# Dense gate weights and a ones row by transfer, and attention values projected per head ahead of the tail

## What is computed

```python
for l in range(4):                       # sLSTM: a recurrence over 256 time steps, 4 layers x 4 heads of 32
    x = x + slstm_layer(ln(x, ln1_w[l]), conv_w[l], conv_b[l], wi[l], wf[l], wz[l], wo[l], rker[l], ...)
    x = x + gelu_ffn(ln(x, ln2_w[l]), ff_up[l], ff_down[l])

q = (x @ Wq).reshape(B, Nq, 16, 64)      # cross attention: 16 heads of 64, 6404 keys of 96 channels
k = (context @ Wk).reshape(B, Nk, 16, 64)
v = (context @ Wv).reshape(B, Nk, 16, 64)
attn = softmax(einsum('bqhd,bkhd->bhqk', q, k) * scale)
out = einsum('bhqk,bkhd->bqhd', attn, v).reshape(B, Nq, 1024) @ Wo + bo

for e in range(8):                       # top-1 routed experts with a capacity
    h = relu(tokens @ W1[e] + b1[e]); y = h @ W2[e] + b2[e]
```

## Time and profile before

| | |
|---|---|
| three runs, median | 4427.65 us |
| profiled execution | 4419.72 us (span 4418.0 us) |
| TensorE busy | 3766.4 us, 85% |
| VectorE busy | 3524.0 us, 80% |
| ScalarE busy | 2774.5 us, 63% |
| GpSimd busy | 1048.1 us, 24% |
| preamble, until the last of its instructions | 52.5 us |
| 10 plain chunks | 67.6 to 832.4 us |
| 28 chunks with attention | 836.2 to 3190.4 us |
| tail, 16 heads | 3289.0 to 4332.8 us |

### The profile page before, as it was taken

How to read it: one execution, slowest core, us unless ns; L and a number is a source line. 1 busy time by engine, 2 the same in 40 slices (tenths; PEclk the granted TensorE clock), 3 DMA queues, 4 the chain that set the end, 5 groups by cost and what they waited for, 6 DMA issues and landing times. The chain is left out here.

```text
span 4418.0 us, 103873 instructions
## 1 busy us (share of the span) xinstructions
PE 3766.4 (85%) x37640; PEld 2179.4 (49%) x37640; DVE 3524.0 (80%) x15928; ACT 2774.5 (63%) x8980; POOL 1048.1 (24%) x1219
## 2 busy tenths in 40 slices
PE   4666666459999999999999999999869999999997
PEld 2433334335445444444544544544426666666666
DVE  6777777688888888888888888888667877877865
ACT  3555555435666666666666666666617777777774
POOL 1000000000000000000000000000038788888883
PEclk7555555558999999999999999999969999999998
DMA  3111111000000000000000000000031121122100
GB/s 85 36 42 40 38 43 35 8 4 2 2 5 2 2 3 3 3 4 3 2 2 4 2 2 3 2 2 3 2 89 32 39 47 36 35 47 44 27 9 25
DMA packets 63160, 90.32 MB, mean 20 GB/s; under 512 B 11284, under 2 KB 58196, under 8 KB 59540
## 3 DMA queue, kind: packets, MB, share of 16 engines
q1 hardware_dynamic: 59468, 79.31, 7.2%
q10 hardware_dynamic: 3176, 4.36, 0.4%
HBM read 53.61 MB, written 28.82 MB: 19 GB/s over the span
## 5 line engine op out<-in xcount | busy, mean ns | idle before, releaser
L1201 PEld LDWEIGHTS G<-st,rec_w 128*128 128x128 f16 x19456 | 606.2, 99 | 960.3 <-DVE st L1372 925.0
L1201 PE MATMUL G<-st,rec_w 128*128 128x1 f16 x19456 | 683.4, 165 | 406.9 <-DVE st L1372 390.2
L1629 POOL TENSOR_TENSOR plt<-pft,pht 128x512 f16<-128x512 f32 x765 | 866.9, 1159 | 227.6 <-DVE pht L1874 156.9
L1153 PE MATMUL OA<-pf,vals 128*97 128x512 f32 (+1 forms) x1632 | 851.0, 602 | 0.6
L1081 ACT ACTIVATE st<-hb 32x16 f16<-32x16 f32 x1216 | 259.0, 213 | 703.0 <-DVE hb L1367 702.4
L130 DVE TENSOR_REDUCE mx<-MT 128x1 f32<-128x512 f32 (+1 forms) x832 | 531.4, 665 | 105.1 <-PE MT L1682 96.4
L1061 ACT ACTIVATE pf<-SC,ln_prob 128x512 f32<-128x512 f32 (+1 forms) x816 | 560.5, 687 | 20.6
L130 DVE TENSOR_REDUCE mx<-MB 128x1 f32<-128x512 f32 (+1 forms) x832 | 537.4, 660 | 41.0 <-PE MB L122 26.3
L1624 ACT ACTIVATE pft<-ST,ln_prob 128x512 f32<-128x512 f32 (+1 forms) x816 | 536.5, 684 | 44.4 <-PE ST L1704 38.0
L1622 ACT ACTIVATE pht<-ST,ln_prob 128x512 f16<-128x512 f32 x510 | 350.4, 687 | 260.8 <-PE ST L1704 253.0
L1072 ACT ACTIVATE tf<-G 32x16 f32<-32x16 f32 x1216 | 212.1, 174 | 393.2 <-PE G L1201 365.7
(11 more groups left out here) (354 smaller groups left out, 6892.5 us busy)
## 6 DMA issues: line engine op xcount, KB each, us to landing
kc<-scr_k SPq DMA_DIRECT2D x32, 816.0 KB, 12.6
scr_k<-k_hl SPq DMA_DIRECT2D x192, 128.0 KB, 1.7
k<-scr_k SPq DMA_DIRECT2D x16, 816.0 KB, 6.5
w<-in_L_ffn_W SPq DMA_DIRECT2D x16, 256.0 KB, 4.6
xin<-x SPq DMA_DIRECT2D x38, 48.0 KB, 1.8
scr_k<-k_hl SPq DMA_DIRECT2D x16, 96.0 KB, 1.6
rnat<-in_L_attn_rker SPq DMA_DIRECT2D x3, 256.0 KB, 6.7
up_w<-in_L_attn_ff_up SPq DMA_DIRECT2D x1, 672.0 KB
```

Source lines behind the costliest of these rows:

```text
L1153: pe.matmul(OA[0:at.DC + 1, :], at.vals[0:rows, i, :], pf[0:rows, tile % 2, :], start=(i == 0), stop=(i == KT - 1)).then_inc(pv_done, 1)
L1201: mm = pe.matmul(g[:, t, c:c + 1], rec_w[:, c, :], st[:, c:c + 1], start=False, stop=(c == C - 1), skip_group_check=True)
L1629: return eng.tensor_tensor(pl[0:k, t % NP_, :], pf[0:k, t % NP_, :], ph[0:k, t % NP_, :], ALU.subtract)
```

## The change

Five parts:

1. The gate weights come as four dense transfers into a tile `dense`, issued first; four ScalarE copies put them onto the diagonal of `nat`. ScalarE's own loads of `Wq`, `Wv`, `Wo` and `post_w` are issued after that. The scaling of `vals` leaves the preamble and is done in the plain chunks, six tiles a chunk.
2. `ByHead` takes the place of `KeysByHead`: the 104 key items and 102 new value items, 21 to a chunk. A value item projects one tile of 128 keys to 8 heads (512 columns); its parts are collected in `v_hl` and stored once per four tiles and half (26 stores of up to 1,032 KB, `scr_v`).
3. The split of `vals` into `vals_c` is gone; `Wv` itself is split once (`wv_h`, `wv_l`). Two places of the weight products move (9 to 22, 23 to 24).
4. In the tail the values are per head (`vc`, one load of 1.7 MB a head, two buffers): the value matmuls have 129 and 65 columns in place of 193 and 97, and the head's output has 64 channels and goes through `Wo` alone. The low parts are still taken two tiles later.
5. The constant row of `k2` is loaded from memory (`scr_one`) in place of the GpSimd memset.

```diff
-    PLACES = (3, 5, 6, 9, 23)
-    T_SPLIT, SPLIT_TILES, T_QUERY = 29, 6, 27
+    PLACES = (3, 5, 6, 22, 24)
+    T_SCALE, SCALE_TILES, T_QUERY, T_PARTS = 16, 6, 27, 26
...
-class KeysByHead:
-
-
-    PLACES = (0, 2, 4, 7, 8, 11, 12, 15, 18, 19, 21)
+class ByHead:
+
+
+    PLACES = (0, 1, 2, 4, 7, 8, 11, 12, 13, 14, 15, 18, 19, 20, 21, 23, 25, 28, 29, 30, 31)
     T_STORE = 18
+    TILES_A_STORE = 4
 
     def __init__(self, at, chunks, chunk_steps):
-        self.pieces = [(c * 512, min(c * 512 + 512, at.KT * P)) for c in range(-(-at.KT * P // 512))]
-        total = at.HEADS // 2 * len(self.pieces)
+        self.chunk_steps = chunk_steps
+        self.keys = [(pair, a0, min(a0 + 512, at.KT * P)) for pair in range(at.HEADS // 2) for a0 in range(0, at.KT * P, 512)]
+        self.values = [(j0 // self.TILES_A_STORE, half, j, j == min(j0 + self.TILES_A_STORE, at.KT) - 1)
+                       for j0 in range(0, at.KT, self.TILES_A_STORE) for half in range(2)
+                       for j in range(j0, min(j0 + self.TILES_A_STORE, at.KT))]
+        self.n_keys, self.total = len(self.keys), len(self.keys) + len(self.values)
+        self.v_stores = 2 * -(-at.KT // self.TILES_A_STORE)
         places = [c * chunk_steps + p for c in range(chunks) for p in self.PLACES]
-        assert total <= len(places)
-        self.at_step = {s: i for i, s in enumerate(places[:total])}
-        self.total = total
-
-    def item(self, i):
-        pair, c = divmod(i, len(self.pieces))
-        return pair, *self.pieces[c]
-
-    def before_store(self, chunk, chunk_steps):
-        return [i for s, i in self.at_step.items() if s // chunk_steps == chunk and s % chunk_steps < self.T_STORE]
-
-    def after_store(self, chunk, chunk_steps):
-        return [i for s, i in self.at_step.items() if s // chunk_steps == chunk and s % chunk_steps >= self.T_STORE]
-
-
-def slstm_stage(nc, x, w, ctx_in, wa, scratch_in, scratch_out, dims, at, first_row, xa_out, keys_out):
+        assert self.total <= len(places)
+        self.at_step = {s: i for i, s in enumerate(places[:self.total])}
+
+    def in_chunk(self, chunk, late):
+        return [i for s, i in self.at_step.items()
...
+                    for g, name in enumerate(("wi", "wf", "wz", "wo")):
+                        sp.dma_start(dense[:, :, g, :], w[name].rearrange("l h o d -> (h o) l d")).then_inc(d_nat, 16)
+                    for dst, src in ((ln1_w[:, :], w["ln1_w"].rearrange("l d -> d l")),
...
-                    sp.wait_ge(z_nat, 1)
-                    for g, name in enumerate(("wi", "wf", "wz", "wo")):
-                        for h in range(H):
-                            sp.dma_start(nat[h * Q:(h + 1) * Q, :, g, h * Q:(h + 1) * Q],
-                                         w[name][:, h, :, :].rearrange("l o d -> o l d")).then_inc(d_nat, 16)
...
-                    pool.memset(at.vals_c[:, :, at.DC:at.DC + 1], 1.0)
...
+                    nc.scalar.preload_act_table_set("exp_and_others")
+                    a.wait_ge(z_nat, 1)
+                    a.wait_ge(d_nat, 16 * 4)
+                    for h in range(H):
+                        ins = s.activation(nat[h * Q:(h + 1) * Q, :, :, h * Q:(h + 1) * Q], dense[h * Q:(h + 1) * Q, :, :, :], ACT.Copy)
+                    ins.then_inc(z_diag, 1)
+                    a.wait_ge(d_wk, 16)
+                    s.activation(at.wk_h[:, :], at.wk_sb[:, :], ACT.Copy).then_inc(wk_hi, 1)
...
-                    nc.scalar.preload_act_table_set("exp_and_others")
-                    a.wait_ge(d_wk, 16)
-                    s.activation(at.wk_h[:, :], at.wk_sb[:, :], ACT.Copy).then_inc(wk_hi, 1)
...
-                    s.activation(at.vals[:, :, 0:at.DC], ctx_f[:, :, 0:at.DC], ACT.Copy, scale=at.C_SCALE)
...
-                    pe.wait_ge(d_nat, 16 * 4 * H)
+                    pe.wait_ge(z_diag, 1)
...
+        v_hl = sb("v_hl", [P, 2, at.HEADS // 2, ByHead.TILES_A_STORE, 2 * at.DHEAD + 1], F16)
...
+                        elif by_head.values[i - by_head.n_keys][3]:
+                            group, half, j, _ = by_head.values[i - by_head.n_keys]
+                            j0, b = group * by_head.TILES_A_STORE, half % 2
+                            heads = slice(half * (at.HEADS // 2), (half + 1) * (at.HEADS // 2))
+                            sp.wait_ge(k_low, i + 1)
+                            sp.dma_start(values_out[heads, :, j0:j + 1, :].rearrange("h p t c -> p h t c"),
+                                         v_hl[:, b, :, 0:j + 1 - j0, :]).then_inc(d_vals[b], 16)
...
+                        sp.dma_start(ones_out, at.keys_h[at.DC:at.DC + 1, :]).then_inc(d_out, 16)
...
+                                    done, b, hi, _, product = value_parts(by_head, i)
+                                    if done >= 2:
+                                        a.wait_ge(d_vals[b], 16 * (done // 2))
+                                    s.activation(hi, product, ACT.Copy).then_inc(k_hi, 1)
...
+                                    rows, cols = slice(j * P, (j + 1) * P), slice(half * 512, (half + 1) * 512)
+                                    out = SC[i % 2][:, :]
+                                    pe.matmul(out, at.keys_l[:, rows], at.wv_h[:, cols], start=True, stop=False)
+                                    pe.matmul(out, at.keys_h[0:at.DC, rows], at.wv_l[:, cols], start=False, stop=False)
+                                    pe.matmul(out, at.keys_h[0:at.DC, rows], at.wv_h[:, cols], start=False,
+                                              stop=True).then_inc(k_full, 1)
...
+                                    _, _, hi, low, product = value_parts(by_head, i)
+                                    v.tensor_tensor(low, product, hi, ALU.subtract).then_inc(k_low, 1)
...
-    VC = 2 * DC + 1
+    VC = 2 * DHEAD + 1
...
+        vc = sb("vc", [P, 2, KT, VC], F16)
...
+                for b in range(2):
+                    sp.dma_start(k2[DHEAD:DHEAD + 1, b, :], ones_in).then_inc(k_one, 16)
+                def load_values(h):
+                    sp.dma_start(vc[:, h % 2, :, :], values_by_head[h, :, :, :]).then_inc(d_vc[h % 2], 16)
+
                 load_keys(0)
                 load_hi(0)
+                load_values(0)
                 load_keys(1)
                 load_hi(1)
                 load_keys(2)
+                load_values(1)
...
+                    sp.wait_ge(pv_done, KT * (g + 1))
+                    load_values(g + 2)
...
-                pool.wait_ge(a_rs, 2)
-                pool.memset(k2[DHEAD:DHEAD + 1, :, :], at.M_ONE).then_inc(k_one, 1)
...
-                        mm = pe.matmul(OA[i // 2][:, (i % 2) * 256:(i % 2) * 256 + DC + 1], pl[0:k, t % NP_, i * P:(i + 1) * P],
-                                       at.vals_c[0:k, j, 0:DC + 1], start=False, stop=(j == KT - 1), skip_group_check=True)
+                        mm = pe.matmul(OA[i // 2][:, (i % 2) * 256:(i % 2) * 256 + DHEAD + 1], pl[0:k, t % NP_, i * P:(i + 1) * P],
+                                       vc[0:k, (t // KT) % 2, j, 0:DHEAD + 1], start=False, stop=(j == KT - 1), skip_group_check=True)
...
-                                  at.vals_c[0:k, j, :], start=(j == 0 and i % 2 == 0), stop=False, skip_group_check=True)
+                                  vc[0:k, g % 2, j, :], start=(j == 0 and i % 2 == 0), stop=False, skip_group_check=True)
```

More of the change, by code:

```diff
@@ L301, in __init__ @@
         places = [c * chunk_steps + p for c in range(chunks) for p in self.PLACES]
-        assert len(steps) <= len(places) and chunks * self.SPLIT_TILES >= at.KT
+        assert len(steps) <= len(places) and chunks * self.SCALE_TILES >= at.KT
         self.at_step = {s: (what, i // 3) for i, (s, what) in enumerate(zip(places, steps))}
-        self.split = {c * chunk_steps + self.T_SPLIT: (c * self.SPLIT_TILES, min((c + 1) * self.SPLIT_TILES, at.KT))
-                      for c in range(chunks) if c * self.SPLIT_TILES < at.KT}
+        self.scale = {c * chunk_steps + self.T_SCALE: (c * self.SCALE_TILES, min((c + 1) * self.SCALE_TILES, at.KT))
+                      for c in range(chunks) if c * self.SCALE_TILES < at.KT}
@@ new lines, in __init__ @@
+        self.n_keys, self.total = len(self.keys), len(self.keys) + len(self.values)
+        self.v_stores = 2 * -(-at.KT // self.TILES_A_STORE)
+        places = [c * chunk_steps + p for c in range(chunks) for p in self.PLACES]
+        assert self.total <= len(places)
+        self.at_step = {s: i for i, s in enumerate(places[:self.total])}
+    def in_chunk(self, chunk, late):
+        return [i for s, i in self.at_step.items()
+                if s // self.chunk_steps == chunk and (s % self.chunk_steps >= self.T_STORE) == late]
@@ L459, in slstm_stage @@
             z_nat = sem("z_nat")
+            z_diag = sem("z_diag")
             z_id = sem("z_id")
@@ L698, in slstm_stage @@
         d_blk, d_xa = sem("d_blk"), sem("d_xa")
-        w_turn, w_turned, w_qk, w_vo, w_kept, v_hi = (
```

(22 more changed lines are left out.)

127 lines of the change are left out of this document (72 added, 55 removed).

## The result

| | before | after |
|---|---|---|
| median of the runs | 4424.13 us (4413.94 to 4432.75, 6 runs) | 4396.86 us (4384.33 to 4408.2, 6 runs) |
| profiled execution, span | 4418.0 us | 4388.7 us |

The ratio is 0.9941, with a 95% interval of 0.9922 to 0.996. The kernel is 27 us faster where 72 were forecast. The stages ahead of the tail's tiles came out near the forecast; the tail's tiles gave half of what they should.

The account below looks back on a forecast made before the run. Bounds: the ring of dependent operations in plain chunks, TensorE in the tail with GpSimd close behind. -8 + 44 - 10.4 - 97 - 1 = -72 from 4419.7 gives 4347; the median, 7.9 above, 4355 us, range 4325 to 4385.

Parts of the forecast that it names:

- plain chunks: The ten chunks without attention: added items lengthen TensorE's, VectorE's and buffer waits, +44 us together, bounds 25 to 65.
- the tail's tiles: Value matmuls of 129 and 65 columns save TensorE 8.4 us a head; 6.5 expected over 15 heads, 97 us.
- Preamble: Before the first plain chunk: earlier gate-weight transfers win 3.9 us and the removed scaling of `vals` 4.3; 8 taken.
- tail start: Before the tail's first tile: without GpSimd's memset four VectorE normalisations no longer take 11.57 us; 10.4 us go.
- the bare low part at the convolution: Plain chunks, step 24: VectorE's convolution ends after the ring's operation starts, so an item's low part adds its full 0.68 us.
- the forecast for TensorE: Plain chunks, t = 28 to 31: items behind gate matmuls exceed TensorE's room, 2.3 us a chunk in nine chunks, 21 us.
- the coupling: Tail: engines holding each other up keep a head at 59.3 us, where TensorE alone as bound would give 57.1.
- The last head: Tail's final head, without maxima, where GpSimd at 56.1 of 58.3 us is the bound: 1 us less.
- tail taken over by VectorE and GpSimd: Rival: the tail's heads stay at 62.5 us, a gain of 50 and a time of 4402; chance 16%.
- Narrow matmuls: Rival: the tail's four 65-column matmuls stay at 0.18 us, losing 3 us a head, 4400 at most; chance 5%.
- clock: Rival: TensorE's clock rises to 2.4 GHz in the plain chunks, 20 to 45 us less, about 4315; chance 8%.
- value stores: Rival: ScalarE waits in the plain chunks for `v_hl` stores landing after 18 us or more, making the kernel slower; chance 4%.

## Why the prediction was wrong

- **Direction and the stages ahead of the tail's tiles: right.** Preamble -8.8 for -8, plain chunks +43.0 for +44, tail start -10.0 for -10.4. The step from ring to ring behind the gates was 3.02 for 2.96, the bare low part at the convolution cost 0.67 for 0.68 (2.98 us for that step, 2.31 with its item moved). Between the ring's first activations, steps 28 to 31 grew by 2.3 us a chunk, which is the forecast for TensorE. The other 2.0 a chunk are the bare low part's and 0.2 to 0.3 at each of five further steps; how much of it is VectorE and how much the buffers was not taken apart.
- **The tail's tiles: the step that failed.** "With maxima, VectorE is at nearly 90% too and its maxima alternate with TensorE over two banks, so I expect 59.3: 6.5 a head". TensorE's own saving was right: 8.4 us a head worked out, 61.8 to 53.4 measured from start to start (8.1 by medians). The term mis-sized was the coupling, what the engines cost each other once TensorE is faster. I took for it the 2.2 us that the last head shows over GpSimd's 56.1, and the last head has no maxima to be held up. TensorE's standing still grew by 5.2 us a head instead (4.0 to 9.1), and a head took 62.56. Without VectorE's low parts a head takes 60.1: that one instruction in sixteen tiles is 2.4 of the 3.3 us missed, shown by leaving it to GpSimd. The other 0.8 stays open. In that kernel TensorE stands still for 6.7 us a head, 1.4 more than before ahead of the maxima's matmuls and 1.0 more ahead of the value matmuls, and no run took these apart.
- **The last head.** The 1 us less that was forecast didn't come (59.6 after 58.3): GpSimd, which bounds it, was busy for 56.0 us as before.
- **What I did not look at:** the low part's own row. In the trace of before it had 908 ns on average where 690 is its length alone, and I had priced VectorE by busy time, in which such a wait counts as work; its place in the queue I didn't price at all.
- **The rival "tail taken over by VectorE and GpSimd"** named 62.5 a head and 4402, and the time was 4396.86; a head above 62.5 was also the prediction's own sign of being wrong. The rival's size was right and its mechanism half: GpSimd did wait for VectorE's high parts (101.5 us, 144.8 before), but less once VectorE's low parts were gone (27.9), and it was not a matter of jitter that buffers could cover (a third tile of slack: 62.49).
- **Narrow matmuls, clock, value stores:** none came true. The clock of the plain chunks was 0.50, 1.2 GHz, over all of their 807.8 us, as before; TensorE was busy for 74% of them (599 us) rather than the nearly 80% of the prediction.

## What to carry to other kernels

When the bound engine gets faster, look in each engine next to it for the rare long instruction ahead of something that others wait for, not for its sum of busy time: 3.2 us a head moved from VectorE to ScalarE brought 0.55, 3.6 us moved away as low parts brought 2.4. A mean duration that lies above the shortest of its kind can be a wait hidden in busy time, and a change elsewhere can make it grow: here from 0.91 to 1.29 us. An idle slot on one engine is a place for work only if every engine that handles that work has one, in the order in which the ring needs them.
